# A GRU over 512 steps: r and m with moving weights in column tiles, z with standing weights, mixing by scans

## The reference

```
def step(h, x_t):
    fused = jax.nn.sigmoid(jnp.concatenate([x_t, h], axis=-1) @ w_W + w_b)
    hidden_state, output_state = jnp.split(fused, 2, axis=-1)
    memory_state = x_t @ wx_W + wx_b + hidden_state * (h @ wh_W + wh_b)
    h_new = output_state * h + (1.0 - output_state) * jnp.tanh(memory_state)
    return (h_new, h_new)
```

## Time and profile before

| | |
|---|---|
| median of 3 runs | 2375.87 us (2370.36 to 2380.26) |
| the profiled execution | 2355.67 us, span 2353.8 us |
| PE, PEld busy | 97%, 97% of the span |
| DVE, ACT, POOL busy | 64%, 43%, 20% |
| chain that ended last | PE 94%, DVE 3% |

### The profile page before, as it was taken

How to read it: one execution, slowest core, us unless ns; L and a number is a source line. 1 busy time by engine, 2 the same in 40 slices (tenths; PEclk the granted TensorE clock), 3 DMA queues, 4 the chain that set the end, 5 groups by cost and what they waited for, 6 DMA issues and landing times.

```text
span 2353.8 us, 181864 instructions
## 1 busy us (share of the span) xinstructions
PE 2293.2 (97%) x76800; PEld 2273.5 (97%) x76800; DVE 1506.0 (64%) x8208; ACT 1017.0 (43%) x5528; POOL 474.9 (20%) x2117
## 2 busy tenths in 40 slices
PE   5999999999999999999999999999999999999988
PEld 5999999999999999999999999999999999999987
DVE  4666666666666666666666666666666666666666
ACT  4444444444444444444444444444444444444433
POOL 0212122122122222221222222222222212222111
PEclk8999999999999999999999999999999999999985
DMA  4210000000000000000000000000000000000000
GB/s 166 72 26 9 9 9 9 4 9 9 9 9 4 9 9 9 9 9 4 9 9 9 9 4 9 9 9 9 9 4 9 9 9 9 4 9 9 9 9 9
DMA packets 37292, 33.16 MB, mean 14 GB/s; under 512 B 1856, under 2 KB 34624, under 8 KB 36672
## 3 DMA queue, kind: packets, MB, share of 16 engines
q1 hardware_dynamic: 36672, 23.10, 3.2%
HBM read 14.70 MB, written 8.39 MB: 10 GB/s over the span
## 4 chain that ended last, share of the span: by engine, by line
PE 94%; DVE 3%; issue 1%; ACT 0%; DMA 0%; SPq 0%; DVEq 0%
PE ps L203 77%; PE ps L191 17%; DVE h L380 1%; DVE zn L364 1%; DVE h L370 0%; DVE h L375 0%; DMA wx<-in_wx_W 0%; DVE m_pre L358 0%; DVE pre L345 0%; ACT n_tanh L297 0%; DVE m_terms L353 0%; SPq L161 0%; ACT wh L313 0%; ACT xg L276 0%; SPq L162 0%
## 5 line engine op out<-in xcount | busy, mean ns | idle before, releaser
L203 PEld LDWEIGHTS ps<-h,wh 128*128 128x128 bf16 x73728 | 1948.3, 96 | 51.8 <-issue 21.7
L203 PE MATMUL ps<-h,wh 128*128 128x24 bf16 x73728 | 1960.6, 174 | 32.6 <-DVE h L380 14.8
L345 DVE TENSOR_REDUCE pre<-ps 128x16 f32<-128x64 f32 x2048 | 456.5, 223 | 509.0 <-PE ps L203 468.8
L289 ACT ACTIVATE r_gate<-pre 128x16 f32<-128x16 f32 x1024 | 221.0, 216 | 829.4 <-DVE pre L345 776.2
L463 POOL TENSOR_TENSOR zh<-z_gate,h 128x16 f32<-128x16 f32 x1024 | 226.9, 222 | 1576.3 <-ACT z_gate L291 1576.3
L191 PE MATMUL ps<-x_sb,wx 128*128 (+1 forms) x3072 | 486.2, 297 | 22.7 <-DMA wx<-in_wx_W 20.2
L191 PEld LDWEIGHTS ps<-x_sb,wx 128*128 128x128 f32 x3072 | 399.0, 199 | 23.1 <-issue 20.2
L297 ACT ACTIVATE n_tanh<-m_pre 128x16 f32<-128x16 f32 x1024 | 220.6, 215 | 286.5 <-DVE m_pre L358 286.5
L358 DVE TENSOR_REDUCE m_pre<-m_terms 128x16 f32<-128x80 f32 x1024 | 305.6, 298 | 17.9 <-issue 0.3
L364 DVE TENSOR_TENSOR zn<-one_minus_z,n_tanh 128x16 f32<-128x16 f32 x1024 | 179.3, 175 | 183.8 <-ACT n_tanh L297 183.8
L291 ACT ACTIVATE z_gate<-pre 128x16 f32<-128x16 f32 x1024 | 221.0, 216 | 170.2 <-DVE pre L345 125.5
(11 more groups left out here) (12 smaller groups left out, 9.9 us busy)
## 6 DMA issues: line engine op xcount, KB each, us to landing
x_sb<-in_x SPq DMA_DIRECT2D x32, 256.0 KB, 3.7
out_h<-y SPq DMA_DIRECT2D x32, 256.0 KB, 2.6
wh_rest<-in_w_W SPq DMA_DIRECT2D x4, 512.0 KB, 7.4
wx<-in_w_W SPq DMA_DIRECT2D x4, 512.0 KB, 7.3
wh_rest<-in_wh_W SPq DMA_DIRECT2D x4, 256.0 KB, 8.7
wx<-in_wx_W SPq DMA_DIRECT2D x4, 256.0 KB, 7.9
h<-in_h SPq DMA_DIRECT2D x1, 16.0 KB, 1.8
bias_x<-in_w_b SPq DMA_DIRECT2D x1, 4.0 KB, 1.9
```

Source lines behind the costliest of these rows:

```text
L203: mm = pe.matmul(ps[:, bank(o, g), ci * SLOTS * B:(ci * SLOTS + PARTS) * B], wh[:, part, k, col:col + P], h_bf[:, :, s - 1 if s else STEPS ...
L289: act.activation(r_gate[:, o, :], pre[:, o, R, :], ACT.Sigmoid).then_inc(r_ready[o], 1)
L345: dve.tensor_reduce(cb(pre[:, o, g, :]), slots(o, g).rearrange("p c s b -> p c b s"), AX.X, ALU.add).then_inc(pre_ready[o][g], 1)
```

## The change

The three products of a step are split in two kinds, and the elementwise work behind them is arranged anew.

- **r and m** swap operands: a part of h (`parts_of`, 128 x 24, its elements 24 bytes apart) stands, and 256 columns of weights (a quarter of r's and of m's) move past it. 24 standing columns fit into 32, so four such matmuls are put into four column tiles of the array (`tile_position=(0, Q * j)`), each writing 32 partitions of one bank. For 4 input chunks and 3 parts that is 12 groups of four, 48 matmuls; half of them may start at `h_ready[0]`.
- Their result has batch and part on the partitions, so DVE turns it by 32x32 blocks (`turn`, one instruction for r, one for m, 128 columns each, PSUM to PSUM), and then adds parts and x part in one reduce for r and one for m over both halves (128 elements in, 32 out).
- **z** keeps standing weights: 48 matmuls of 24 columns behind the r and m products. ACT first copies h's parts without gaps into `h_moving` (`move_h`, two copies of 48 elements), and PE waits for `h_moved`.
- r*m + x is one scan on each half (`mix_m`, 32 elements: factors 0, r and addends hm, xm). z*(h-n)+n, with n the tanh, is one scan on each half (`mix_h`, 48 elements: factors 0, -1, z over n, h, n), written into a layout with three places for each value. That drops 1-z on ACT, z*h on POOL, and `scale_n` and `write_h` on DVE. tanh is written twice (32 elements).
- POOL places both halves of m's x part after both `m_pre_ready`, and adds the output in four instructions of 64 elements instead of one of 256.
- The 48 x products of a block stand behind its first 15 steps, 3 or 4 in each, and the separate 8 columns of step 0 are dropped. The weights come in one DMA a chunk, laid out on the host. DVE clears PSUM and the h store at the start. Where an instruction has several waits, the order puts `tanh_ready`, `r_ready` and `rm_done` in the instruction itself.

```diff
+        def terms(g):
+            return ps[:, R_TERMS + g, 0:KC * PITCH].rearrange("p (c w) -> p c w", w=PITCH)
+        def mid(part, s, o):
+            at = 1 + part * REGION
+            return h[:, s, o, at:at + REGION].rearrange("p (i w) -> p i w", w=TRI)[:, :, 1]
+        h_bf = h[:, :, :, :].bitcast(BF16)
+        def mid_top(part, s, o):
+            at = 2 * (1 + part * REGION)
+            return h_bf[:, s, o, at:at + 2 * REGION].rearrange("p (i w) -> p i w", w=2 * TRI)[:, :, 3]
+        def parts_of(s, k):
+            o, ci = divmod(k, HC)
+            at = 2 * (1 + TRI * ci + 1) + 1
+            step = 2 * TRI * HC
+            return h_bf[:, s, o, at:at + step * (PARTS * B - 1) + 1:step]
+        def by_chunk(a, slot):
+            return a[:, :, :, slot].rearrange("p o (b c) -> p o c b", c=HC)
+        def both_parts_of(s, o):
+            at = 2 * (1 + 1) + 1
+            step = 2 * TRI
+            return h_bf[:, s, o, at:at + step * (PARTS * HB - 1) + 1:step].rearrange("p (i c) -> p c i", c=HC)
+        def z_slots(o):
+            return ps[:, Z_BANK + o, 0:HC * SLOTS * B].rearrange("p (c s b) -> p c s b", c=HC, s=SLOTS)
...
+            def rm_products(ks, s):
+                for k in ks:
+                    for part in range(PARTS):
+                        for j in range(TILES):
+                            mm = pe.matmul(ps[Q * j:Q * j + PARTS * B, RM_BANK, 0:RM],
+                                           parts_of(s - 1 if s else S, k),
+                                           wh[:, part, k, j * RM:(j + 1) * RM],
+                                           start=(k == 0 and part == 0),
+                                           stop=(k == KC - 1 and part == PARTS - 1),
+                                           tile_position=(0, Q * j))
+                return mm
+            def z_products(o):
+                for ci in range(HC):
+                    col = 2 * D + (HC * o + ci) * P
+                    for k in range(KC):
                         for part in range(PARTS):
...
+                            mm = pe.matmul(ps[:, Z_BANK + o, ci * SLOTS * B:(ci * SLOTS + PARTS) * B],
+                                           wh[:, part, k, col:col + P], h_moving[:, k // HC, k % HC, :],
                                            start=(ci == 0 and k == 0 and part == 0),
                                            stop=(ci == HC - 1 and k == KC - 1 and part == PARTS - 1),
                                            skip_group_check=True)
                 return mm
...
                 nxt = held(pe, t0 + (s + 1))
                 pe.wait_ge(h_ready[0], nxt)
...
+                rm_products(range(HC), s)
                 pe.wait_ge(h_ready[1], nxt)
...
+                rm_products(range(HC, KC), s).then_inc(rm_done, 1)
+                pe.wait_ge(h_moved, nxt)
+                pe.wait_ge(xz_placed, nxt)
+                for o in range(HALVES):
+                    z_products(o).then_inc(z_done[o], 1)
...
+            def place_xr(which, s):
+                act.activation(terms(R)[:, :, 0:B], xg[:, which, s, R].rearrange("p a c b -> p (a c) b"), ACT.Copy)\
+                    .then_inc(xr_placed, 1)
+            def place_xz(which, s):
+                dst = ps[:, Z_BANK:Z_BANK + HALVES, 0:HC * SLOTS * B] \
+                    .rearrange("p o (c s b) -> p o c s b", c=HC, s=SLOTS)[:, :, :, PARTS, :]
+                src = xg[:, which, s, Z].rearrange("p a (o c) b -> p (a o) c b", c=HC)
+                act.activation(dst, src, ACT.Copy).then_inc(xz_placed, 1)
+            def update(o, nxt):
+                act.wait_ge(z_summed[o], nxt)
+                act.activation(h_by[:, o, :, 2].rearrange("p (b c) -> p c b", c=HC), pre_z[:, o, :, :], ACT.Sigmoid)\
+                    .then_inc(z_ready[o], 1)
+            def new(o, s, nxt):
+                act.wait_ge(m_pre_ready[o], nxt)
+                n_twice = h[:, s - 1 if s else S, o, 1:1 + REGION].rearrange("p (i w) -> p i w", w=TRI)[:, :, 0::2]
+                act.activation(n_twice, m_pre[:, o, :, 1].unsqueeze(2).to_broadcast([P, HB, 2]), ACT.Tanh)\
+                    .then_inc(tanh_ready[o], 1)
+            def move_h(o, s, count):
+                act.wait_ge(h_ready[o], count)
+                return act.activation(h_moving[:, o, :, :], both_parts_of(s, o), ACT.Copy)
...
+                act.wait_ge(r_summed, nxt)
+                act.activation(by_chunk(m_by, 1), pre_r[:, :, :].rearrange("p (o c) b -> p o c b", c=HC), ACT.Sigmoid)\
+                    .then_inc(r_ready, 1)
+                update(0, nxt)
+                new(0, s, nxt)
+                update(1, nxt)
+                new(1, s, nxt)
+                if s < S:
+                    place_xr(this, s + 1)
+                    place_xz(this, s + 1)
                 elif not last:
...
+                    place_xr(other, 0)
+                    place_xz(other, 0)
+                if s < S or not last:
+                    nxt2 = held(act, t0 + (s + 2))
+                    move_h(0, s, nxt2)
+                    move_h(1, s, nxt2).then_inc(h_moved, 1)
+                if not last:
+                    for u in X_ENDS[s]:
                         empty(u, other, unit0)
...
+            def turn(g, done):
+                dve.transpose(terms(g)[:, :, B:B + Q],
+                              ps[:, RM_BANK, g * P:(g + 1) * P].rearrange("p (c q) -> p c q", q=Q)).then_inc(done, 1)
+            def summed(g):
+                return terms(g)[:, :, 0:(1 + PARTS) * B].rearrange("p c (s b) -> p c b s", b=B)
+            def sum_z(o, nxt):
+                dve.wait_ge(z_done[o], nxt)
+                dve.tensor_reduce(pre_z[:, o, :, :], z_slots(o).rearrange("p c s b -> p c b s"), AX.X, ALU.add)\
+                    .then_inc(z_summed[o], 1)
+            def mix_m(o):
+                dve.tensor_tensor_scan(m_pre[:, o].rearrange("p i w -> p (i w)"),
+                                       m_by[:, o].rearrange("p i w -> p (i w)"),
+                                       m_add[:, o].rearrange("p i w -> p (i w)"), 0.0, ALU.mult, ALU.add)\
+                    .then_inc(m_pre_ready[o], 1)
+            def mix_h(o, s, nxt):
                 dve.wait_ge(tanh_ready[o], nxt)
...
+                dve.wait_ge(z_ready[o], nxt)
+                dve.tensor_tensor_scan(h[:, s, o, 0:REGION], h_by[:, o].rearrange("p i w -> p (i w)"),
+                                       h[:, s - 1 if s else S, o, 1:1 + REGION], 0.0, ALU.mult, ALU.add)\
                     .then_inc(h_written[o], 1)
...
                     dve.wait_ge(y_late, held(dve, i + 1))
...
+                dve.wait_ge(rm_done, nxt)
+                dve.wait_ge(xr_placed, nxt)
+                turn(R, r_turned)
+                turn(M, m_turned)
+                dve.wait_ge(r_turned, nxt)
+                dve.tensor_reduce(pre_r[:, :, :], summed(R), AX.X, ALU.add).then_inc(r_summed, 1)
+                dve.wait_ge(m_turned, nxt)
+                dve.tensor_reduce(by_chunk(m_add, 0), summed(M).rearrange("p (o c) b s -> p o c b s", c=HC),
+                                  AX.X, ALU.add).then_inc(hm_summed, 1)
+                sum_z(0, nxt)
+                dve.wait_ge(r_ready, nxt)
+                dve.wait_ge(hm_summed, nxt)
+                dve.wait_ge(xm_placed, nxt)
+                mix_m(0)
+                sum_z(1, nxt)
+                mix_m(1)
+                mix_h(0, s, nxt)
                 write_rest1(0, s, nxt)
...
                 write_rest2(0, s, nxt)
...
+                mix_h(1, s, nxt)
                 write_rest1(1, s, nxt)
                 write_rest2(1, s, nxt)
...
+            def place_xm(which, s):
+                for o in range(HALVES):
+                    placed = pool.tensor_copy(m_add[:, o, :, 1].rearrange("p (b c) -> p c b", c=HC),
+                                              xg[:, which, s, M, HC * o:HC * (o + 1), :]
+                                              .rearrange("p a c b -> p (a c) b"))
+                placed.then_inc(xm_placed, 1)
...
+                for c in range(KC):
+                    o, ci = divmod(c, HC)
+                    xs = x_sb[:, c, cols:cols + Y_HALF * B] if isinstance(cols, int) else \
+                        x_sb[:, c, bass.ds(cols, Y_HALF * B)]
+                    at = 1 + TRI * ci + 1
+                    hs = h[:, s0:s0 + Y_HALF, o, at:at + TRI * HC * (B - 1) + 1:TRI * HC]
+                    last = pool.tensor_tensor(y[:, c, s0:s0 + Y_HALF, :], xs.rearrange("p (t b) -> p t b", b=B), hs, ALU.add)
+                last.then_inc(early_or_late, 1)
```

342 lines of the change are left out of this document (130 added, 212 removed).

## The result

The changed kernel takes **2035.38 us** (median of 4 runs, 2033.49 to 2036.86); the kernel before took 2373.11 us beside it (2367.79 to 2380.26). The ratio is 0.8575, with a 95% interval of 0.8548 to 0.8601. The forecast was 2183 us with 2060 as the lowest: the direction was right, and the gain was underestimated by 148 us.

The account below looks back on a forecast made before the run. PE, busy 97%, was taken as the bound, DVE's chain next. Steps of 3.98 us plus output add and stalls gave 66.2 a block, 2114 for 511 steps; with both ends and the median's 20, 2183 us, range 2060 to 2500.

Parts of the forecast that it names:

- PE's part from `h_ready[0]` to the turn: r and m products: 12 groups at 0.114 us, half startable at `h_ready[0]`; DVE's first turn starts 1.09 after `h_ready[1]`.
- the sum: A loop step: 1.09 to the turn, 2.79 on DVE and ACT, 0.10 for POOL, 3.98 us against 4.37.
- tiles overlap: Rival on r and m products: tiles don't overlap at all, 4.1 us a step more, some 4280 us; chance 0.05.
- pairs are issued fast enough: Rival in `rm_products`: tiled pairs issued too slowly, slower above 0.145 us a group, 2710 at 50 ns a pair; chance 0.15.
- DVE's chain isn't longer: Rival: turns, scans, reduces and POOL near upper bounds, +0.3 to +0.7 us a step, 2335 to 2540 us; chance 0.16.
- leave the clock at full: Rival: PE waits each step and its clock falls to half through the loop, 2850 us; chance 0.04.
- One sign: Sign expected in the profile if right: the chain that ended last lies mostly on DVE.
- stalls and half-clock stretches today: Loss per block of 16 steps: 2.3 us today less some 0.5 of the add; 1.8 kept.
- the listed bounds: Per-step ranges for group, turns, scans, reduces, tile switching and POOL, such as -0.08 to +0.43 us for the group.
- POOL's output add: Four POOL instructions meeting two rests twice a block: 0.7 us a block, bounds 0 and 2.4.
- The copies of POOL beside the rests: POOL's two copies of 0.20 us beside `mix_h(0)` and its rests: 0.10 us a step, between 0 and 0.3.
- the median: Median of the runs, put 20 us above the profiled execution of 2163: 2183 us.

Follow-up runs that it names:

- experiment 8: 12 long-met waits a step added on PE: to the kernel before, 2563.34 us (ratio 1.0854); to the changed kernel, 2121.07 us.
- z_gaps: The changed kernel without the `move_h` copies, z's products moving h itself with its 24-byte gaps: 2690.44 us, ratio 1.1396.
- before_x_mid: The kernel before with one of each step's three x products moved from the step's end to its middle: 2427.72 us, ratio 1.0309.

## Why the prediction was off

**What held.** The mechanism and its parts. A group takes 0.109 us (forecast 0.114), PE's part from `h_ready[0]` to the turn 1.64 (1.67), PE is busy 90% of the span (80 to 90 forecast), the copies `move_h` and the emptying on ACT are hidden. The scans take 0.22 and 0.245 (0.22 and 0.25), the reduce of r 0.25 (0.29), the turn 0.33 (0.29). The step is 3.88 where the sum gave 3.98. The four rivals didn't come: tiles overlap, pairs are issued fast enough, DVE's chain isn't longer, and PE's waits of 0.29 in most steps leave the clock at full. One sign didn't come either: the chain that ended last lies 71% on PE and 21% on DVE, where most of it was forecast on DVE.

**The step that failed** is "stalls and half-clock stretches today are 2.3 less some 0.5 of the add; I keep 1.8". It is 0 in the changed loop: 0.11 us a step, 58 us. The loss was carried over without a cause, and the listed bounds held nothing for it, so the sum had no way down to what came. In the kernel before, this excess is 67 us over 511 steps of 4.38. By its trace 31 us of it lie in 37 steps that touch a stretch at half clock, 15 in the last step of each block (0.5 each), 15 in the other steps of the loop, 5.6 where the loop is left, and 1 in the last block. One of its sources can be seen at work there: PE runs out of instructions, and the clock then halves. Its timeline and two windows (us, busy us and matmuls, granted clock, DMA):

```profile
231.53 3.73 PE L203 MATMUL ps<-h,wh 128*128 128x24 bf16 x142
235.85 0.20 PE L203 MATMUL ps<-h,wh 128*128 128x24 bf16 x2 [0.60 <-issue]
```

```profile
232.00:235.00 3.00, 3.00 (x126) 1.00 0.02 5
236.40:239.60 3.20, 3.20 (x100) 0.50 0.02 5
```

Two matmuls short of the step's end PE stops for 0.60 us, and behind it the granted clock is 0.50, the lower of the two levels. 19 packets at 3.77 us are 71.6 us a block, 4.48 a step; by its work alone it would take 4.38. By that estimate 0.10 of the 0.13 over goes with the supply of instructions. That the kernel before stands at this limit is shown by experiment 8, where met waits alone lengthened its steps. The share of 0.10 is argued: the profile calls only 14.6 us of PE's idle time "issue". Nor is a lack of instructions all that brings half clock. z_gaps, with 13 packets a block and 1.1 us of such idle time, ran 439 us at half clock, and before_x_mid kept most of its stretches with hardly a pause for issue. Why the changed loop has none is open. The changed kernel needs 13 packets a block and is far from this limit. The Trainium skill (Runtime: NRT & Kernel Launch, Instruction fetch mechanics) describes the blocks of 16 KiB and calls their cost mostly hidden; for small matmuls this trace disagrees, at one packet in 3.77 us.

**Three smaller terms.** POOL's output add was charged 0.7 us a block and costs 0: its trace shows

```profile
1061.40 0.19 DVE L397 TENSOR_TENSOR h<-h 128x16 f32<-128x16 f32 x1
1061.54 1.29 POOL L485 TENSOR_TENSOR y<-x_sb,h 128x64 f32<-128x64 f32 x4 [0.58 <-DVE h L386]
...
1062.61 0.53 DVE L365 STREAM_TRANSPOSE ps<-ps 128x128 f32<-128x128 f32 x2 [1.02 <-PE ps L218]
```

that it starts as the last rest ends and fills DVE's wait for PE. That was 22 us over the run. The copies of POOL beside the rests were charged 0.10 a step; L397 takes 0.196 beside them and 0.188 without, so 0.02 at most. With PE's part 0.03 shorter than forecast, and DVE's own 0.01 longer, this makes the 0.10 between 3.98 and 3.88, 53 us. And the median was set 20 us over the profiled run, as in the kernel before; now it is 1.5 below it: 21 us. 58 + 22 + 53 + 21 are 154.

Against that stand 5.7 us, which leave the 148 that were missing: 4.6 in the two steps where the loop is left, and 1.2 in two steps of the last block, where DVE stops for 1.08 us (the other steps of that block are slightly shorter). They are what is left of the carried-over 1.8 a block, since the kernel before lost 5.6 at the same place; they had no term of their own. The exit and DVE's stop in the timeline, and windows of PE:

```profile
1962.30 2.76 PE L218 MATMUL ps<-wh,h 128*24 128x256 bf16 x46 [1.74 <-issue]
...
1991.44 0.29 DVE L412 TENSOR_REDUCE m_add<-ps 128x32 f32<-128x128 f32 x1 [1.08 <-issue]
```

```profile
1940.00:1957.00 17.00, 15.77 (x440) 1.00 0.02 4
1962.00:1971.00 9.00, 7.66 (x172) 0.50 0.12 33
1973.00:2020.00 47.00, 33.59 (x1148) 1.00 0.02 4
```

PE stops for 1.74 us for "issue", runs some 9 us at half clock, and is back at full without any x products beside it. In the earlier trace rows the last block ran at half to its end, so here too the changed kernel does better than one would read from before.

## What to carry to other kernels

When matmuls are small, count the instructions as well as their columns: look at the packets of the instruction queue a loop pass, and take a pause marked "issue" in the middle of PE's work as a sign that instructions may be lacking; added waits that are long met test it. An excess over the steady step must be split by place and given a cause before it is carried into a forecast; here all of it but the exit was gone from the changed kernel. And when two edits do little alone, look whether each is hidden behind the other before dropping both.
